# A residual conditioning kernel on one core: W_e's first slices loaded singly, fewer warm-up products, a head stage in another order

## What is computed

```
x: (128, 128, 512)   cond: (128, 512)   W_proj, W_u, W_e: (512, 512)   b_proj: (512)
u      = gelu(cond @ W_proj + b_proj)              # 128 x 512
logits = (u @ W_u)[:, None, :] + x @ W_e           # per batch row and position
out    = x + logits  =  x @ (W_e + I) + (u @ W_u)[:, None, :]
```

## Time and profile before

| what | value |
|---|---|
| time, median of 3 runs | 344.18 us (343.98 to 346.36) |
| the profiled execution's own time | 344.53 us |
| its span, first to last instruction | 342.4 us |
| PE busy | 338.1 us, 99% of the span |
| DVE, ACT, POOL busy | 263.6, 249.1, 283.7 us (77%, 73%, 83%) |
| DMA queue 1 | 70.53 MB, 81.5% of the 16 engines' span |
| granted TensorE clock | full in all 40 slices of the page |

### The profile page before, as it was taken

One profiled execution on the slowest core, in us unless ns is written; L12 is line 12 of the kernel. 1 busy time (PEld: TensorE's weight loads), 2 busy tenths in 40 slices (PEclk: granted clock), 3 DMA queues, 4 the chain that ended last, 5 costly groups with the idle time before them and its releaser, 6 DMA issues.

```text
span 342.4 us, 7876 instructions
## 1 busy us (share of the span) xinstructions
PE 338.1 (99%) x2703; PEld 329.7 (96%) x2703; DVE 263.6 (77%) x302; ACT 249.1 (73%) x428; POOL 283.7 (83%) x203
## 2 busy tenths in 40 slices
PE   8999999999999999999999999999999999999996
PEld 4869999999999999999999999999999999999996
DVE  2989997777887777887777789777788877778811
ACT  3677787778777777877777877777787777787741
POOL 2499999988889898889898888989888888888860
PEclk9999999999999999999999999999999999999999
DMA  7998799878888977888997787898878799787216
GB/s 260 314 196 211 167 235 242 232 200 215 200 184 199 241 219 198 209 204 169 230 230 219 195 214 184 184 245 217 217 186 222 175 208 245 202 208 205 92 48 231
DMA packets 73353, 70.64 MB, mean 206 GB/s; under 512 B 2944, under 2 KB 68480, under 8 KB 69248
## 3 DMA queue, kind: packets, MB, share of 16 engines
q1 hardware_dynamic: 73344, 70.53, 81.5%
HBM read 36.96 MB, written 33.55 MB: 206 GB/s over the span
## 4 chain that ended last, share of the span: by engine, by line
PE 98%; DMA 1%; ACT 0%; issue 0%
PE banks L857 31%; PE banks L861 30%; PE banks L859 30%; PE banks L783 2%; PE banks L825 2%; PE banks L843 1%; DMA head_raw<-in_x 1%; PE banks L768 1%; PE banks L764 1%; PE banks L821 0%; PE banks L818 0%; PE banks L815 0%; ACT y L597 0%
## 5 line engine op out<-in xcount | busy, mean ns | idle before, releaser
L857 PE MATMUL banks<-t_hi,hi 128*128 128x256 f32 x496 | 140.6, 283 | 0.1
L861 PE MATMUL banks<-t_hi,lo 128*128 128x256 f32 x496 | 140.4, 283 | 0.0
L859 PE MATMUL banks<-t_lo,hi 128*128 128x256 f32 x496 | 140.4, 283 | 0.0
L857 PE MATMUL banks<-w_hi,hi 128*128 128x256 f32 x372 | 105.4, 283 | 0.0
L859 PE MATMUL banks<-w_lo,hi 128*128 128x256 f32 x372 | 105.3, 283 | 0.0
L861 PE MATMUL banks<-w_hi,lo 128*128 128x256 f32 x372 | 105.3, 283 | 0.0
L602 DVE STREAM_TRANSPOSE work<-quad_raw 128x1024 f32<-128x1024 f32 (+1 forms) x62 | 100.6, 1623 | 0.0
L857 PEld LDWEIGHTS banks<-t_hi,hi 128*128 128x128 f32 x496 | 95.2, 192 | 0.3 <-issue 0.2
L859 PEld LDWEIGHTS banks<-t_lo,hi 128*128 128x128 f32 x496 | 95.2, 192 | 0.0
L861 PEld LDWEIGHTS banks<-t_hi,lo 128*128 128x128 f32 x496 | 95.2, 192 | 0.0
L353 POOL TENSOR_TENSOR lo<-work,hi 128x1024 fp32r<-128x1024 f32 x31 | 75.0, 2418 | 16.9 <-ACT hi L454 16.9
(11 more groups left out here) (81 smaller groups left out, 411.4 us busy)
## 6 DMA issues: line engine op xcount, KB each, us to landing
out<-y SPq DMA_DIRECT2D x31, 1024.0 KB, 4.5
quad_raw<-in_x SPq DMA_DIRECT2D x120, 256.0 KB, 5.7
w_e<-in_L_cond_weight_matrix SPq DMA_DIRECT2D x2, 512.0 KB, 5.9
w_proj_sb<-in_L_cond_W_proj SPq DMA_DIRECT2D x2, 512.0 KB, 7.9
w_u<-in_L_cond_weight_matrix SPq DMA_DIRECT2D x1, 1024.0 KB, 8.5
quad_raw<-in_x SPq DMA_DIRECT2D x8, 128.0 KB, 8.1
out<-y SPq DMA_DIRECT2D x3, 256.0 KB, 2.2
head_raw<-in_x SPq DMA_DIRECT2D x1, 512.0 KB, 3.7
```

The lines of the kernel that those rows point to most:

```text
L857: pe.matmul(psum[:, t, :], a_hi[:, 2 * j + t, :], b_hi[:, j, :], start=False, stop=False, skip_group_check=True)
L859: pe.matmul(psum[:, t, :], a_hi[:, 2 * j + t, :], b_lo[:, j, :], start=False, stop=False, skip_group_check=True)
L861: last = pe.matmul(psum[:, t, :], a_lo[:, 2 * j + t, :], b_hi[:, j, :], start=False, stop=(j == T - 1), skip_group_check=True)
```

## The change

- W_e comes in three transfers in place of two: slice 0, slice 1 (256 KB each), then slices 2 and 3 together.
- POOL makes, in the storage of bias that is not used yet, a 128 x 512 array first_eye that holds slice 0's part of the identity (a memset and an affine_select, 128 x 512). DVE then makes slice 0's high part in one operation, w_e + first_eye, instead of adding the identity and then rounding. The diagonal of slice 0 in W_e itself gets its identity later, on POOL, behind slice 1's; the low parts of W_e wait for it.
- The second set of warm-up products has two instead of eight.
- PE's 24 direct products of chunk 0 stand in another order: the first tile's low product goes ahead of slice 1's high products, and from there on slice j+1's high products come behind the low products of W_e's slice j-1 (low_w).
- DVE makes quad 0's S3 behind S1's low part and the first evacuate, and ACT rounds S3 behind b_bank's seeding.

```diff
-WARM_ON = 8
+WARM_ON = 2
...
+        first_eye = bias[:, :]
...
-            def load_w_e(n):
-                sp.dma_start(w_e[:, 2 * n:2 * n + 2, :], w_e_dram[:, 2 * n:2 * n + 2, :]).then_inc(w_e_loaded[n], 16)
+            def load_w_e(n, slices):
+                sp.dma_start(w_e[:, slices, :], w_e_dram[:, slices, :]).then_inc(w_e_loaded[n], 16)
 
             sp.dma_start(direct, x[:, 0:T, :]).then_inc(direct_loaded, 16)
-            for n in range(2):
-                load_w_e(n)
+            load_w_e(0, slice(0, 1))
+            load_w_e(1, slice(1, 2))
+            load_w_e(2, slice(2, NJ))
...
+            pool.memset(first_eye, 0.0).then_inc(first_eye_zeroed, 1)
+            pool.wait_ge(first_eye_zeroed, 1)
+            pool.affine_select(out=first_eye, in_=first_eye, compare_op=ALU.not_equal, fill=1.0,
+                               base=0, pattern=[[-1, C]], channel_multiplier=NJ).then_inc(first_eye_ready, 1)
...
-            for j in range(1, NJ):
-                pool.wait_ge(w_e_loaded[j // 2], 16)
+
+            def add_ident(j, done):
                 diag = diagonal(j)
-                pool.tensor_tensor(diag, diag, ident[:, :], ALU.add).then_inc(w_diag_ready, 1)
+                pool.tensor_tensor(diag, diag, ident[:, :], ALU.add).then_inc(done, 1)
+
+            pool.wait_ge(w_e_loaded[1], 16)
+            add_ident(1, w_diag_ready)
+            pool.wait_ge(w_hi_ready[0], 1)
+            add_ident(0, first_diag_ready)
+            pool.wait_ge(w_e_loaded[2], 16)
+            for j in range(2, NJ):
+                add_ident(j, w_diag_ready)
...
                 if early:
+                    hi_s3(k, p, True)
                     snap_c(k, p, first)
...
-            hi_s3(0, 0, True)
             period(0, 0, True, True)
...
-            dve.wait_ge(ident_ready, 1)
+            dve.wait_ge(first_eye_ready, 1)
             dve.wait_ge(w_e_loaded[0], 16)
-            first_diag = diagonal(0)
-            dve.tensor_tensor(first_diag, first_diag, ident[:, :], ALU.add).then_inc(first_diag_ready, 1)
-            dve.wait_ge(first_diag_ready, 1)
-            dve.tensor_copy(w_hi[:, 0, :], w_e[:, 0, :]).then_inc(w_hi_ready[0], 1)
+            dve.tensor_tensor(w_hi[:, 0, :], w_e[:, 0, :], first_eye, ALU.add).then_inc(w_hi_ready[0], 1)
             split_direct(0)
             split_direct(1)
+            dve.wait_ge(first_diag_ready, 1)
...
             sum_s1(0, 0, True)
-            sum_s3(0, 0, True)
...
             evacuate(0, slice(0, 1))
+            sum_s3(0, 0, True)
             evacuate(0, slice(1, T))
```

More of the change, by code:

```diff
@@ L151, in build_cond_residual @@
         b_proj_loaded = sem("b_proj_loaded")
-        w_e_loaded = [sem(f"w_e_loaded{n}") for n in range(2)]
+        w_e_loaded = [sem(f"w_e_loaded{n}") for n in range(3)]
         direct_loaded = sem("direct_loaded")
@@ L177, in build_cond_residual @@
         w_diag_ready = sem("w_diag_ready")
+        first_eye_zeroed = sem("first_eye_zeroed")
+        first_eye_ready = sem("first_eye_ready")
         first_diag_ready = sem("first_diag_ready")
@@ L790, in high, with low, low_w @@
                     product(t, x_hi[0], w_hi, j, first=(j == 0))
-            high(0)
-            for j in range(NJ + 1):
+            def low(j, t):
+                if j == 0:
+                    pe.wait_ge(direct_lo_ready, t + 1)
+                product(t, x_lo[0], w_hi, j)
+            def low_w(j, last=False):
+                pe.wait_ge(w_lo_ready[j], 1)
+                for t in range(T):
+                    end = product(t, x_hi[0], w_lo, j, last=last)
+                return end
+            high(0)
+            low(0, 0)
+            high(1)
+            low(0, 1)
+            for j in range(1, NJ):
+                for t in range(T):
+                    low(j, t)
+                if j == NJ - 1:
+                    pe.wait_ge(cond_loaded, 16)
+                    flip(flip_psum, by_j(cond_sb[:, :]), cond_flipped)
+                low_w(j - 1)
                 if j + 1 < NJ:
                     high(j + 1)
[L797 to L809, removed]
+            low_w(NJ - 1, last=True).then_inc(multiplied, 1)
             pe.wait_ge(cond_hi_ready, 1)
```

## The result

| | before | changed |
|---|---|---|
| median of 15 runs | 345.02 us (343.98 to 346.93) | 347.14 us (346.27 to 349.69) |
| the profiled execution, its span | 344.53, 342.4 us | 346.54, 344.2 us |

The ratio is 1.0061, with a 95% interval of 1.0039 to 1.0083. The medians differ by 2.1 us and the two profiled spans by 1.8.

A forecast was written before the change was run, and what follows sets the result against it. PE, busy 338.1 of 342.4 us, was taken to bound the kernel. -0.66 us at 8 us, +0.35 at u_t and +0.31 at quad 1's m5 gave 0.0, so 344.2 us; range 343.7 to 345.0.

The forecast's parts named there:

- The forecast's chain: DVE and ACT's operations up to quad 1's m5: its end at 36.50 us stays, so PE's lead is given back.
- its step on the loads: DVE's transposes at 19.09 and 21.52 us are held by loads the change does not hasten, so they stay.
- the rival of the later load: Load for DVE's transpose at 21.52 us lands later, nothing to 0.45 us, passed on to the end; up to 344.6; chance 0.18.
- Slice 0 alone at 5.74: W_e's slice 0 is released at 5.74 us, where the pair came at 6.74; its high part runs 5.74 to 6.42.
- Three products, then a wait for slice 1: PE's direct products start at 6.7 us; three run, PE idles about 0.7 us, continues at 8.15; at most 0.66 us won.
- A lead of 0.31 at the product with W_u: PE's product with W_u starts at 19.76 instead of 20.07 us; the DVE and ACT chain leaves 0.31 us of lead.
- The lead given back at quad 1's m5: PE reaches quad 1's m5 0.31 us earlier but waits for S1's low part, which still ends at 36.50 us.
- S3's place and POOL's first_eye: Moving S3 leaves quad 1's first transpose at 28.48 us; POOL's first_eye operations, 2.4 us for both, are hidden.
- The clock: Rival: TensorE's clock falls or rises later near 7.4 to 8.1 us, 24 direct products cost +4.8 us; 348.7; chance 0.04.

The follow-up runs named there:

- e10: The changed kernel with slice j of W_e taken from contiguous rows 128 j to 128 j + 127; 344.86 us against 344.57, ratio 1.0001.
- e4: The kernel before with W_e in two 512 KB transfers, slices 0 and 2, then 1 and 3; 347.60 us against 344.44, ratio 1.0089.
- e11: The changed kernel with slices 0 and 1 in one transfer and chunk 0's second evacuate behind quad 1's S1 low part; 345.04 us, ratio 1.0021.
- e3: The kernel before with slices 0 and 1 loaded as partitions 0 to 63, then 64 to 127; 346.91 us against 344.44, ratio 1.0069.
- e6: The kernel before with W_proj in four transfers of one slice each; 344.96 us against 344.58, ratio 1.0011.
- e2: The kernel before with only W_e's loads changed: slice 0, slice 1, then slices 2 and 3; 348.12 us against 344.44, ratio 1.0120.

## Why the prediction was wrong, step by step

**The forecast's chain held, but its step on the loads failed, and the rival that covers it had a price four times too small.** The forecast said that the transposes at 19.09 and 21.52 "are held by loads that the change does not hasten" and left them where they were; that the change delays them was left to a rival. They came at 21.03 and 23.37. The time went by the rival of the later load. Its mechanism was put as "each 0.1 us by which this load lands later is 0.1 us at 36.50 and at the end", and so it was in the first pair of profiles: 1.85 us at the load, 1.81 at m5 and 1.8 at the end. What failed is its price. The step reads: "nothing, if the full queue hides it, and one issue on SP, 0.89 / 2 = 0.45 us", and "Nearest to the case is nothing, since the queue is full". I bounded a change of access pattern by what an issue costs, and took the bytes of a full queue to move at one rate whatever they are. The measured term is 1.65 (the second pair of profiles) to 1.85 us, and so the range ended at 345.0 where 347.1 was measured. 0.84 us of the distance to the forecast's 344.2 is not the change: 344.18 was the median of three runs of the kernel before, and over 15 it is 345.02.

A hint was in the trace of before: its queue ran at 291 GB/s between 4 and 6 us, while W_e's first pair was read, and at 412 in the two microseconds behind it. Why the first read with gaps was slow could have been asked. It would not have given the price, since the second pair, which leaves out as much, was read mostly in that faster stretch.

**Slice 0 alone at 5.74.** Landed at 6.29, its operation started at 6.39, so 0.35 us were won of the forecast 1.0. Where the slice is contiguous (e10) it started at 5.38. The one operation took 0.69 (0.68 forecast) and was followed at once by the low parts.

**Three products, then a wait for slice 1.** PE's first product was at 7.14 (6.7 forecast), the fourth at 8.38 (8.15). In e10, where the loads were near what the forecast took them for, these were 6.67 and 7.96. The forecast counted from 8.12, the chain's row; by PE's timeline the kernel before starts its first direct product at 7.79, so the start moved by 0.65 us in the changed kernel and 1.12 in e10, not 1.4. Three products stood ahead of the wait, as expected, and what PE lost there was, at a pitch of 0.229 us, 0.55 and 0.60 us (0.7 forecast). But in the changed kernel the direct products met a second wait, as slices 2 and 3 landed at 8.7 instead of 7.9; PE waited for slice 2's high part until 10.58. This is the eleventh product, not the twelfth as I had counted; the forecast had called it covered:

```profile
9.91 1.14 ACT L441 CAST w_hi<-w_e 128x512 fp32r<-128x512 f32 x2 [1.58 <-POOL w_e L343]
10.58 0.73 PE L801 MATMUL banks<-w_hi,hi 128*128 128x512 f32 x2 [0.31 <-ACT w_hi L441]
...
13.50 1.14 ACT L444 CAST hi<-w_proj_sb 128x512 fp32r<-128x512 f32 x2 [1.12 <-DMA w_proj_sb<-in_L_cond_W_proj]
```

**A lead of 0.31 at the product with W_u.** In the changed kernel it was at 21.75, 1.68 later than before, because W_proj's casts were 1.97 later. In e10 it was at 19.94, 0.13 earlier than before and not 0.31: the chain over u_t takes the lead, as said, and took more of it than said.

**The lead given back at quad 1's m5.** Seen in e10 as it was forecast: PE reaches m1's end early, stands idle, and starts m5 right behind S1's low part, whose DVE row ends at 36.03 + 0.68 = 36.71.

```profile
36.23 0.28 PE L886 MATMUL banks<-w_hi,lo 128*128 128x256 f32 x1
36.76 0.39 PE L882 MATMUL banks<-t_hi,hi 128*128 128x256 f32 x1 [0.25 <-DVE lo L681]
```

Its ratio of 1.0001 (0.9987 to 1.0015, so within about half a microsecond) is the forecast's "0.0 us". So no worth of the local gain can be seen at the end; that the loads stay where they are was the error.

**S3's place and POOL's first_eye.** Seven operations between S1 and quad 1's transpose took 4.65 us after (25.64 to 30.29) and 4.66 before (23.82 to 28.48): no cost, no gain. The first_eye operations were hidden: slice 0's high part waited for its load, 5.25 us, and not for them.

**The clock.** The rival's fall did not come: the granted clock is 1.00 from the direct products on. Its later rise did, without a cost. The two warm-up products of the changed kernel took 1.06 us, those of e10 0.59:

```profile
5.92 1.06 PE L782 MATMUL banks<-zeros 128*128 128x512 bf16 x2
```

```profile
6.25 0.59 PE L782 MATMUL banks<-zeros 128*128 128x512 bf16 x2
```

The first row is the changed kernel, still at 1.2 GHz by its pitch (the window's clock column shows 1.00 there too, so ahead of the rise the pitch has to be read). They ended before slice 0's high part was ready at 6.39 + 0.69 = 7.08 us, so nothing waited for them. A fall of the clock is seen in another run. In e4, which has eight warm-up products, PE had 1.40 and 0.95 us of work in the two stretches of 2 us from 6 on, and at about 10.7 the granted clock fell to 0.50, the 1.2 GHz level. Between 10.7 and 14.0 us, two direct products take about 0.85 us instead of 0.46:

```profile
8.00:10.00 2.00, 0.95 (x3) 0.48 (x4) 2.00 (x4) 0.99 (x2) 1.55 (x3) 1.00 0.97 305
10.70:14.00 3.30, 3.30 (x9) 2.58 (x8) 2.81 (x6) 2.30 (x5) 0.00 (x0) 0.50 1.19 263
```

```profile
7.89 0.73 PE L783 MATMUL banks<-w_hi,hi 128*128 128x512 f32 x2 [0.60 <-DVE w_hi L703]
9.68 0.73 PE L783 MATMUL banks<-w_hi,hi 128*128 128x512 f32 x2 [1.05 <-ACT w_hi L421]
...
10.75 1.05 PE L783 MATMUL banks<-w_hi,hi 128*128 128x512 f32 x2
11.60 1.05 PE L783 MATMUL banks<-w_hi,lo 128*128 128x512 f32 x2
```

The Trainium skill states in "TensorE: Matmul & The Clock Gate", Part 1, "The HAM clock gate", that an idle stretch brings the half rate back. That the half rate can come back in the middle of a kernel is seen in e4; that one idle stretch does it is not, since e4's gaps were 0.60 and 1.05 us. In e11 PE stood idle for 1.45 us in one piece ahead of its first direct product, and the clock stayed at 1.00. Between 6 and 10 us PE was busy for 2.56 us in e11 and for 2.35 in e4, so these rows do not say what makes the difference. The row of e11, from PE's timeline:

```profile
7.54 0.73 PE L801 MATMUL banks<-w_hi,hi 128*128 128x512 f32 x2 [1.45 <-DVE w_hi L719]
```

**What stays open.** Why e3 was slow is not explained by the gaps: its pieces were those of the kernel before, but each transfer served only half of the partitions. Its first landings were no wider than the changed kernel's (4.92 to 7.30 for the two halves, 4.39 to 7.01 for the two slices), but its W_u was the widest of all, 16.42 to 20.80. That the engines' getting out of step at 5 us is what makes the load at 21 us late was argued from the landings and not tested by itself. Nor is it known what in the memory makes the first read with gaps slow, or why W_proj's slices in e6, as far apart, cost less.

## What to carry to other kernels

A transfer is priced by how it lies in main memory as well as by its bytes. Here, splitting a load so that a first part comes earlier made everything behind it in the queue late where the parts were interleaved in main memory, and made nothing measurably late where they were contiguous. Before an early part is split off, look for the first place behind it at which an engine waits for that queue; there the lateness came through one to one here, and the local gain did not. Where two chains meet, a gain on one is worth nothing until the other is shortened, and in the runs here the next meeting place held it then.

## What the runs showed of the hardware that I had not expected

W_e's 1 MB in one contiguous transfer landed at 6.75 us, 0.12 later than half of it did in the kernel before (6.63; 6.37 in its second profile), whose first pair skips every second 4 KB: 418 against 291 GB/s in the stretch from 4 to 6 us. With single slices, 2 KB of every 8, it was 217 (228 in e2), with single contiguous slices of the same pieces 343. The engines' landings were 0.4, 1.1 and 1.9 us wide, and the width was still there in W_u more than 10 us later (1.08 before, 2.23 after). The second pair, with the same gaps as the first, was read at full speed: 163 ns for a 4 KB piece where the first pair's took 221. A transfer over 64 partitions twice instead of 128 once went with a delay of 3.3 us at quad 0's second transpose (24.81 against 21.52), in one profiled execution.
